# Second expert weights split by GpSimd, route weights formed once: one core, cross attention and mixture of experts

## The chip, the cores and the metric

One core of one Trainium2 chip runs the whole program. The metric is the device time in microseconds, of which three runs were made: median 615.03 us, from 614.83 to 616.17. The engines are TensorE (PE, with its weight loads PEld), VectorE (DVE), ScalarE (ACT), GpSimd (POOL) and SyncE (SP), which issues most transfers. They run side by side and order each other by semaphores; each works through its own instructions in their order.

## The reference, cut to what matters

The input x is 4 x 1024 rows of 256. Four blocks follow each other, each added to x with a tanh gain:

```
x = x + tanh(g_xattn[0]) * attention(layernorm(x), ctx, ctx, mask)     # 77 keys
x = x + tanh(g_ffn[0])   * moe(layernorm(x))                           # below
x = x + tanh(g_xattn[1]) * attention with projections, softmax over queries
x = x + tanh(g_ffn[1])   * gated feed-forward with integer weights

# moe, for xt = all 4096 rows
logits = xt @ gate_w.T + gate_b
scores = softmax(logits)
top_w, top_i = top_k(scores, 2)              # 8 experts, two for each row
y = sum over the two: top_w * ((silu(xt @ w1.T + b1) * (xt @ w3.T + b3)) @ w2.T + b2)
z = silu(xt @ ws1.T + bs1) * (xt @ ws3.T + bs3) @ ws2.T + bs2     # the shared expert
```

## The kernel before, in words

The rows are worked in 8 groups of 512 (NG = 8, GT = 4 tiles of 128 rows). Every product of the experts is made of three matmuls in a short format: each factor is split into a high part (a rounded copy, made by ScalarE with `copy`) and a low part (the rest, made by a subtraction), and high*high, high*low and low*high are added (`three`).

**Steps.** A loop over g = 1..7 (`step`, one function of this name on each engine) works at two groups together: the shared expert and the routing of group f = g - 1, and the first attention and second layer norm of group g, with the scores of group g + 1. The order on each engine is written out by hand. At the end of a step ScalarE runs, in this order: `hidden_high(f, 3)`, `route_exp(f)` (exp of 36 differences of logits per row, L891), `t2_copy(g)` (the high part of the transposed normed rows, n2Th), `softmax(g + 1)` (four Exp activations with a sum, L835), `expert_high(g)` (the high part of the second weights of expert g, w2h). The next step begins with `silu` (L861), then `pt_copy` (probsT), on which TensorE's `values` (L1294) waits. TensorE runs between its transposes `t2` (L1303) and those `values`: the rest of `down(f)`, then `up(0)`, `probs_t` (L1287, which waits for all probs), in some steps a small setup product, and `up(1)`.

VectorE ends a step with `row_max`, `t2_low`, `shared_out`, `ln1_stats(g + 2)`, then `route_c(f)` (five small instructions, L2084 to L2092: sum, reciprocal, gain, second weight, copy into gate_all) and `expert_low(g)` (L1943, w2l = stage - w2h, 128x512; in step 1 for experts 0 and 1). The next step begins with `prob_scale` (L1974), which needs the sums of the softmax, `hidden(f, 0)` and `residual1` (L2018), which needs `values`.

GpSimd in a step: `rstd_second(g)` (L601 and L604; nb2, on which ScalarE's `ln2_apply`, L815, waits), four scatters by indirect DMA, `rstd_first(g + 2)`, four more scatters. SyncE loads the three `stage` buffers in turn; the next load into one waits for the low part made from its contents (`low_done`).

**Behind the steps** comes the routing of the last group with tables of the expert tiles, then 40 expert tiles (31 of two row tiles, 9 of one), in which TensorE, ScalarE and VectorE work in a loop over u and GpSimd adds the bias (L674). gate_all is read only after them, by `x2`. b2 and b13 are loaded into the place of the buffers of the steps, `stage` among them.

**Activation tables.** In the program as compiled an ACT_TABLE_LOAD stands before an activation whose function is not in the loaded set; the profile shows it under the line of that activation. Exp and Silu lie in different sets, Copy and Identity in both.

Of the kernel before, what the change touches and what calls it, by code (L numbers as in the profile page):

```python
# [7 lines left out]
NE, F = 8, 256  # L8
SF, LF = 512, 768
DH, NH = 16, 16  # L10
P = 128
KD = D // P
T = B * S
GT = 4
NG = T // (P * GT)
# [32 lines left out]
def flamingo_kernel(nc, i, out):  # L48
    ctx = ExitStack()
    with ctx:  # L50
        sems = {}

        def sem(name):
            if name not in sems:
                sems[name] = ctx.enter_context(nc.semaphore(name))
            return sems[name]
# [64 lines left out]
        row_shift = keep.put("row_shift", [P, NE], F32)  # L121
        gate_all = keep.put("gate_all", [P, NG, 2, GT], F32)
        tile_expert = keep.put("tile_expert", [1, NU], I32)
        tile_row = keep.put("tile_row", [1, 2, NU], I32)
# [45 lines left out]
        top8i = w1.put("top8i", [P, GT, 8], U32)  # L170
        dlog = w1.put("dlog", [P, GT, NE + 1], F32)
        elog = w1.put("elog", [P, GT, NE + 1], F32)
        esum = w1.put("esum", [P, GT], F32)
        onehot = w1.put("onehot", [P, 2, GT, NE], F32)
# [3 lines left out]
        rsel = w1.put("rsel", [P, 2, GT, NE], F32)  # L178
        gatew = w1.put("gatew", [P, 2, GT], F32)
        pos = [w1.put(f"pos{p}", [P, 2, GT], U32) for p in range(2)]  # L180
# [174 lines left out]
        def _(sp):  # L355
            def small(dst, src, name="small_in"):
                sp.dma_start(dst, src).then_inc(sem(name), 16)
# [133 lines left out]
            sp.wait_ge(sem("u_done"), MS * NG)  # L491
            sp.wait_ge(sem("gate_done"), NG)
            small(b2, i["b2"].partition_broadcast(P), "b2_in")
            store_mid(7, 1)
# [6 lines left out]
            sp.wait_ge(sem("shared_done"), pairs(NG))  # L501
            sp.wait_ge(sem("route_kept"), 3 * NG)
            for u in range(NU):
# [53 lines left out]
        def _(pool):  # L557
# [57 lines left out]
            def shared_low(c, n):  # L615

                pool.wait_ge(sem(f"high_done{c % 3}"), n)
                pool.tensor_tensor(wsl[:, c, :], stage[c % 3], wsh[:, c, :], ALU.subtract).then_inc(sem(f"low_done{c % 3}"), 1)

            def scatter(f, p, ks=(0, 1), tiles=range(GT)):  # L620

                pool.wait_ge(sem("pos_done"), f + 1)
                for k in ks:
                    for j in tiles:
                        pool.indirect_dma_start(  # L625
                            out=xs, out_offset=bass.IndirectOffsetOnAxis(ap=pos[p][:, k, j:j + 1], axis=0),
                            in_=n2[p][:, j, :], in_offset=None).then_inc(sem(f"scattered{p}"), 16)
# [12 lines left out]
            rstd_first(0)  # L640
# [59 lines left out]

            pool.wait_ge(sem("route_kept"), 3 * NG)
            pool.wait_ge(sem("row_shift_done"), 1)
# [93 lines left out]
        def _(act):  # L796
# [120 lines left out]
            def step(g, p, nxt=True):  # L917
# [80 lines left out]
            silu(f, 3)  # L998
            route_exp(f)
            hidden_high(f, 3)  # L1000
# [246 lines left out]
        def _(pe):  # L1247
# [456 lines left out]

            pe.wait_ge(sem("table_done"), 3)
            experts = {0: expert_of(0)}
            tx(0)
# [196 lines left out]
        def _(dve):  # L1904
# [39 lines left out]

            def expert_low(g):
                low_part(g % 3, w2h[:, g, :], w2l[:, g, :], g // 3 + 3)

            def hidden_low(f, m):
# [114 lines left out]
            def route_a2(f):  # L2063
                dve.wait_ge(sem("top_done"), GT * (f + 1))
                m0 = top8[:, :, 0:1]
                tt(dlog[:, :, 0:NE], logit, m0.broadcast_to([P, GT, NE]), ALU.subtract)
                tt(dlog[:, :, NE:NE + 1], top8[:, :, 1:2], m0, ALU.subtract).then_inc(sem("dlog_done"), 1)

# [11 lines left out]

            def route_c(f):

                dve.wait_ge(sem("elog_done"), f + 1)
                dve.tensor_reduce(esum, elog[:, :, 0:NE], AX.X, ALU.add).then_inc(sem("weights_step"), 1)  # L2084
                dve.wait_ge(sem("weights_step"), 4 * f + 1)
                dve.reciprocal(esum, esum).then_inc(sem("weights_step"), 1)
                dve.wait_ge(sem("weights_step"), 4 * f + 2)
                ts(gatew[:, 0, :], esum, gains[:, 2:3], None, ALU.mult).then_inc(sem("weights_step"), 1)
                dve.wait_ge(sem("weights_step"), 4 * f + 3)
                tt(gatew[:, 1, :], gatew[:, 0, :], elog[:, :, NE], ALU.mult).then_inc(sem("weights_step"), 1)  # L2090
                dve.wait_ge(sem("weights_step"), 4 * f + 4)
                cp(gate_all[:, bass.ds(f, 1), :, :].rearrange("p a k j -> p (a k j)"), gatew.rearrange("p k j -> p (k j)"))\  # L2092
                    .then_inc(sem("route_kept"), 1)

# [23 lines left out]
            def step(g, p, nxt=True, more=True):  # L2118
# [175 lines left out]
            shift_kept()  # L2294
            route_c(f)
            weights_low(0)
# [45 lines left out]
            for u in range(NU + 1):  # L2342
                if u == KINDS.index("S"):
                    dve.wait_ge(sem("b13_in"), 16)
                if u < NU:
                    gated(u)
                if u < NU and not pair(u):
                    gated_single(u)
                if u + 2 < NU:
                    weights_low(u + 2)  # L2350
                if u and not pair(u - 1):
                    hidden_low_of(u - 1)
                if u + 2 < NU:
                    rows_low(u + 2)
                if u < NU and pair(u):
                    hidden_low_of(u)


# [115 lines left out]
            dve.wait_ge(sem("y_mm_done"), NU)  # L2474
            dve.wait_ge(sem("route_kept"), 3 * NG)

# [250 lines left out]
```

## Time and profile before

| | |
|---|---|
| median of three runs | 615.03 us |
| the profiled execution's own time | 614.06 us |
| its span, first to last instruction | 612.3 us |
| mean granted TensorE clock | 0.989 |
| busy: PE, PEld | 572.5 us (94%), 472.6 us (77%) |
| busy: DVE, ACT, POOL | 453.4 us (74%), 376.6 us (62%), 255.8 us (42%) |
| chain that ended last, by engine | PE 60%, DVE 18%, issue 7%, ACT 5% |

Busy time is the sum over an engine's instructions; matmuls are pipelined and their ends are modelled, so a busy PE is not PE at its peak. The chain is followed back from the last instruction, at each step to what released it. In a timeline a row gives the start, the duration, the engine, the line, the operation, the tiles and shapes and the count; in brackets stands how long the engine had been idle and what ended that. The steps lie between about 30 and 160 us of the span, the expert tiles between about 193 and 366 us.

### The profile page before, as it was taken

The page shows a single profiled execution, that of the slowest core. Times are in us where ns is not written, and L with a number is a line of the kernel's source. Part 1 is how long each engine was busy: PE and PEld are TensorE (multiplying, and loading weights), DVE is VectorE, ACT ScalarE, POOL GpSimd, SP SyncE. Part 2 cuts the span into 40 slices and gives each one's busy share as a digit, 9 for nine tenths or more (in the row PEclk, how much of TensorE's full clock was granted, in tenths as well). Part 3 has the DMA queues.
Part 4 walks back from the last instruction along what each step waited for, and adds up shares of the span by engine and source line. Part 5 has one row for each costly group of instructions (what it writes and reads, how often), then busy time and mean ns, then how long its engine had stood idle before and what let it go on. Part 6 is the DMA issues. An engine that isn't in the chain of part 4 may idle for free.

```text
span 612.3 us, 12917 instructions
## 1 busy us (share of the span) xinstructions
PE 572.5 (94%) x3956; PEld 472.6 (77%) x3956; DVE 453.4 (74%) x1246; ACT 376.6 (62%) x729; POOL 255.8 (42%) x284
## 2 busy tenths in 40 slices
PE   7889999998989999999999999699889989999997
PEld 7788889886769999999999988486645645655654
DVE  5888888885645877787798753567888798877755
ACT  5576777873435777777687653155574674684643
POOL 4445565553540235543353346577534650410100
PEclk9899999998999999999999999799999999999999
DMA  7334564441239768887988727632212340200000
GB/s 214 115 110 161 198 208 161 168 166 44 104 138 302 270 234 278 280 257 238 310 239 260 239 79 271 215 122 68 60 34 70 98 127 35 70 1 35 35 36 34
DMA packets 46005, 93.15 MB, mean 152 GB/s; under 512 B 6686, under 2 KB 15978, under 8 KB 45682
## 3 DMA queue, kind: packets, MB, share of 16 engines
q1 hardware_dynamic: 37868, 74.34, 35.9%
q0 software_dynamic: 7344, 17.97, 9.8%
q8 instruction: 33, 0.54, 0.4%
q14 instruction: 34, 0.28, 0.1%
q10 hardware_dynamic: 726, 0.02, 0.1%
HBM read 61.32 MB, written 32.17 MB: 153 GB/s over the span
## 4 chain that ended last, share of the span: by engine, by line
PE 60%; DVE 18%; issue 7%; ACT 5%; another core or an unknown queue 3%; DMA 3%; POOL 2%; SPq 2%; ACTq 0%; DVEq 0%; POOLq 0%
PE bank L1310 11%; PE bank L1308 11%; PE bank L1309 11%; PE bank L1809 6%; PE bank L1830 2%; DVE st L2385 2%; PE bank L1831 2%; PE bank L1652 2%; DMA wraw<-in_wexp 2%; DVE g3l L2462 2%; DVE xa L2376 2%; PE bank L1277 2%; DVE sl L2457 2%; PE bank L1294 2%
## 5 line engine op out<-in xcount | busy, mean ns | idle before, releaser
L625 POOL DMA_INDIRECT rows_by_expert<-n,pos x64 | 64.4, 1006 | 52.6 <-DVE pos L2113 36.1
L674 POOL TENSOR_TENSOR yg<-yg,b 128x512 f32<-128x512 f32 x31 | 46.4, 1498 | 93.9 <-ACT yg L798 93.9
L722 POOL DMA_INDIRECT yr<-expert_out,out_row x64 | 65.7, 1026 | 28.0 <-issue 19.4
L1809 PE MATMUL bank<-m4Th,wint 128*128 128x512 f16 x192 | 69.0, 380 | 5.3 <-DVE sl L2457 3.3
L1308 PE MATMUL bank<-xTh,wph 128*128 128x256 f32 x248 | 72.6, 293 | 1.1 <-DVE wpl L2278 1.0
L1310 PE MATMUL bank<-xTh,wpl 128*128 128x256 f32 x248 | 70.1, 283 | 0.0
L1309 PE MATMUL bank<-xTl,wph 128*128 128x256 f32 x248 | 70.0, 282 | 0.0
L1809 PE MATMUL bank<-m4Tl,wint 128*128 128x512 f16 x192 | 68.8, 379 | 0.0
L2278 DVE TENSOR_TENSOR wpl<-wraw,wph 128x1024 fp32r<-128x1024 f32 x40 | 49.0, 1225 | 14.7 <-ACT wph L798 14.5
L798 ACT ACTIVATE wph<-wraw 128x1024 fp32r<-128x1024 f32 x40 | 42.3, 1058 | 17.6 <-DMA wraw<-in_wexp 9.2
L2457 DVE SCALAR_TENSOR_TENSOR sl<-bank,sl 128x512 f32<-128x512 f32 x48 | 33.1, 689 | 22.5 <-ACT sl L1113 22.4
L1308 PEld LDWEIGHTS bank<-xTh,wph 128*128 128x128 f32 x248 | 47.4, 191 | 1.6 <-DVE wpl L2278 1.2
L1309 PEld LDWEIGHTS bank<-xTl,wph 128*128 128x128 f32 x248 | 47.5, 191 | 0.0
L1310 PEld LDWEIGHTS bank<-xTh,wpl 128*128 128x128 f32 x248 | 47.4, 191 | 0.0
L1830 PE MATMUL bank<-wint,g3h 128*128 128x256 f16 x192 | 42.9, 273 | 1.3 <-DVE g3l L2462 0.8
L1113 ACT ACTIVATE sl<-bank 128x512 f32<-128x512 f32 x48 | 28.3, 589 | 25.2 <-PE bank L1809 24.5
L1831 PE MATMUL bank<-wint,g3l 128*128 128x256 f16 x192 | 42.8, 272 | 0.0
L1308 PE MATMUL bank<-w2h,hTh 128*128 x142 | 40.2, 283 | 1.4 <-DVE hTl L2334 1.4
L1809 PEld LDWEIGHTS bank<-m4Th,wint 128*128 128x128 f16 x192 | 18.3, 98 | 29.1 <-DVE sl L2457 7.9
L1066 ACT ACTIVATE n<-xa,nb,rs 128x256 f32<-128x256 f32 x64 | 34.1, 589 | 10.9 <-DVE nb L2402 10.5
L1310 PE MATMUL bank<-w2h,hTl 128*128 x142 | 40.2, 283 | 0.0
L1309 PE MATMUL bank<-w2l,hTh 128*128 x142 | 40.2, 283 | 0.0
(351 smaller groups left out, 1753.8 us busy)
## 6 DMA issues: line engine op xcount, KB each, us to landing
wraw<-in_wexp SPq DMA_DIRECT2D x40, 512.0 KB
xg<-rows_by_expert SPq DMA_DIRECT2D x31, 256.0 KB, 4.0
expert_out<-yg SPq DMA_DIRECT2D x31, 256.0 KB, 2.9
x_shared<-x SPq DMA_DIRECT2D x8, 512.0 KB
xa<-x_shared SPq DMA_DIRECT2D x4, 1024.0 KB
out<-ost SPq DMA_DIRECT2D x8, 512.0 KB, 2.8
xin<-in_x SPq DMA_DIRECT2D x7, 512.0 KB, 3.8
stage<-in_wexp SPq DMA_DIRECT2D x8, 256.0 KB
```

What stands on the lines that cost most here:

```text
L625: pool.indirect_dma_start(out=xs, out_offset=bass.IndirectOffsetOnAxis(ap=pos[p][:, k, j:j + 1], axis=0), in_=n2[p][:, j, :], in_offset=No ...
L674: pool.tensor_tensor(yg[u % 3], yg[u % 3], b2[:, bass.ds(e, 1), :].broadcast_to([P, 2, D]), ALU.add)\
L722: pool.indirect_dma_start(out=yr[:, c, k, j, :], out_offset=None, in_=ys, in_offset=bass.IndirectOffsetOnAxis(ap=out_row[:, b * GB + c, k, ...
L798: return act.activation(dst, src, ACT.Copy)
L1308: mm(o, ah, bh, start=first, stop=False)
L1309: mm(o, ah, bl, start=False, stop=False)
L1310: return mm(o, al, bh, start=False, stop=final)
L1809: last = mm(bank[:, 2 * (m % 2) + w, :], wt[:, k, m * P:(m + 1) * P], part[c][:, k, :], start=(q == 0 and k == 0), stop=(q == 1 and k == K ...
L1830: mm(bank[:, j, 0:D], g3h[:, k, t], wdv[:, k, :], start=(k == 0), stop=False)
L1831: last = mm(bank[:, j, 0:D], g3l[:, k, t], wdv[:, k, :], start=False, stop=(k == ML - 1))
L2278: tt(wpl[u % 2], wraw[u % 3], wph[u % 2], ALU.subtract).then_inc(sem("low_done0"), 1)
L2457: stt(sl3[n % 3], bank[:, 2 * (m % 2) + 1, :], HID_SCALE, sl3[n % 3], ALU.mult, ALU.mult).then_inc(sem("g3_done"), 1)
```

## The change

The subtraction that makes w2l moves from the end of VectorE's step to the end of GpSimd's step. The route weights are no longer made group by group: `dlog` and `esum` get room for all eight groups, the differences are kept, one Exp activation over all 288 values per row stands where the last group's stood, in place, and four VectorE instructions (`route_weights`) behind tile u = 2 of the expert tiles write gate_all. So ScalarE has no `route_exp` in a step any more. SyncE, TensorE and VectorE get a few waits: b2's load and the first expert tile wait for the low parts, the first low parts of the tiles for those that GpSimd made on the same semaphore. The count of route_kept falls from three to two a group.

```diff
@@ gpsimd
+            def expert_low(g):
+                pool.wait_ge(sem(f"high_done{g % 3}"), g // 3 + 3)
+                pool.tensor_tensor(w2l[:, g, :], stage[g % 3], w2h[:, g, :], ALU.subtract).then_inc(sem(f"low_done{g % 3}"), 1)
...
                 scatter(f, 1 - p, (1,), first)
                 scatter(f, 1 - p, (1,), second)
+                if g == 1:
+                    expert_low(0)
+                expert_low(g)
@@ scalar
-            def route_exp(f):
-                act.wait_ge(sem("dlog_done"), f + 1)
-                act.activation(elog, dlog, ACT.Exp).then_inc(sem("elog_done"), 1)
+            def route_exp():
+                act.wait_ge(sem("dlog_done"), NG)
+                every = dlog.rearrange("p g j e -> p (g j e)")
+                act.activation(every, every, ACT.Exp).then_inc(sem("elog_done"), 1)
...
                 if g == 1:
                     expert_high(0)
-                route_exp(f)
                 t2_copy(g, (0,))
                 t2_copy(g, (1,))
...
             silu(f, 3)
-            route_exp(f)
+            route_exp()
             hidden_high(f, 3)
@@ vector
-            def route_c(f):
-                dve.wait_ge(sem("elog_done"), f + 1)
-                dve.tensor_reduce(esum, elog[:, :, 0:NE], AX.X, ALU.add).then_inc(sem("weights_step"), 1)
...
+            def route_weights():
+                dve.wait_ge(sem("elog_done"), 1)
+                dve.tensor_reduce(esum, dlog[:, :, :, 0:NE], AX.X, ALU.add).then_inc(sem("weights_step"), 1)
+                dve.wait_ge(sem("weights_step"), 1)
+                dve.reciprocal(esum, esum).then_inc(sem("weights_step"), 1)
+                dve.wait_ge(sem("weights_step"), 2)
+                ts(gate_all[:, :, 0, :], esum, gains[:, 2:3], None, ALU.mult).then_inc(sem("weights_step"), 1)
+                dve.wait_ge(sem("weights_step"), 3)
+                tt(gate_all[:, :, 1, :], gate_all[:, :, 0, :], dlog[:, :, :, NE], ALU.mult).then_inc(sem("weights_step"), 1)
...
-                route_c(f)
-                if g == 1:
-                    expert_low(0)
-                expert_low(g)
                 if g == 2:
...
             def weights_low(u):
                 dve.wait_ge(sem("high_done0"), EARLY[0] + u + 1)
+                dve.wait_ge(sem("low_done0"), EARLY[0] + u)
...
             shift_kept()
-            route_c(f)
             weights_low(0)
...
                     hidden_low_of(u)
+                if u == 2:
+                    route_weights()
@@ sync
+            for c in range(3):
+                sp.wait_ge(sem(f"low_done{c}"), EARLY[c])
             small(b2, i["b2"].partition_broadcast(P), "b2_in")
@@ tensor
             pe.wait_ge(sem("table_done"), 3)
+            for c in (1, 2):
+                pe.wait_ge(sem(f"low_done{c}"), EARLY[c])
```

## Rows read from the trace of the kernel before

**Rows 1.** Costliest groups on ScalarE by form, 0 to 190 us: busy us, mean ns
```profile
L861 ACT ACT_TABLE_LOAD x8 | 10.3, 1283 | 0.1
L891 ACT ACT_TABLE_LOAD x8 | 10.3, 1283 | 0.1
```

**Rows 2.** Timeline of ScalarE at the turn to step 6: start us, us
```profile
113.38 1.28 ACT L891 ACT_TABLE_LOAD   x1
...
114.81 1.07 ACT L798 ACTIVATE n2Th<-bank 128x512 fp32r<-128x512 f32 x2
...
117.24 0.23 ACT L835 ACTIVATION_READ_ACCUMULATOR probs<-bank,negmax,rstd 128x1 f32 x1
...
118.01 1.28 ACT L861 ACT_TABLE_LOAD   x1
...
119.71 0.58 ACT L798 ACTIVATE probsT<-bank 77x512 f32<-77x512 f32 x1
```

**Rows 3.** Timeline of TensorE at the same turn
```profile
113.45 1.03 PE L1303 MATMUL bank<-ident,n 128*128 128x128 f32 x8
...
117.85 0.60 PE L1287 MATMUL bank<-ident,probs 128*77 128x128 f32 x4
...
120.34 1.99 PE L1294 MATMUL bank<-ctxr,probsT 77*128 77x256 f32 x8 [0.65 <-ACT probsT L798]
```

**Rows 4.** Timeline of VectorE at the same turn
```profile
118.88 0.16 DVE L2084 TENSOR_REDUCE esum<-elog 128x4 f32<-128x32 f32 x1
...
120.43 0.17 DVE L1974 RECIPROCAL pscale<-psums 128x4 f32<-128x4 f32 x1
...
121.61 1.74 DVE L2018 SCALAR_TENSOR_TENSOR x<-bank,pscale,xin 128x256 f32<-128x256 f32 x4 [0.32 <-PE bank L1294]
```

**Rows 5.** ScalarE, turn to step 2
```profile
41.96 1.06 ACT L798 ACTIVATE n2Th<-bank 128x512 fp32r<-128x512 f32 x2
...
44.39 0.22 ACT L835 ACTIVATION_READ_ACCUMULATOR probs<-bank,negmax,rstd 128x1 f32 x1
```

**Rows 6.** TensorE, turn to step 2
```profile
40.42 1.03 PE L1303 MATMUL bank<-ident,n 128*128 128x128 f32 x8
...
44.96 0.60 PE L1287 MATMUL bank<-ident,probs 128*77 128x128 f32 x4
```

**Rows 7.** ScalarE, turn to step 3
```profile
62.86 0.23 ACT L835 ACTIVATION_READ_ACCUMULATOR probs<-bank,negmax,rstd 128x1 f32 x1
```

**Rows 8.** TensorE, turn to step 3
```profile
63.74 0.60 PE L1287 MATMUL bank<-ident,probs 128*77 128x128 f32 x4
```

**Rows 9.** ScalarE, turn to step 4
```profile
83.63 0.59 ACT L798 ACTIVATE probsT<-bank 77x512 f32<-77x512 f32 x1
```

**Rows 10.** TensorE, turn to step 4
```profile
84.28 1.99 PE L1294 MATMUL bank<-ctxr,probsT 77*128 77x256 f32 x8
```

**Rows 11.** TensorE, turn to step 5
```profile
102.37 0.92 PE L1294 MATMUL bank<-ctxr,probsT 77*128 77x256 f32 x3 [0.17 <-ACT probsT L798]
```

**Rows 12.** ScalarE, turn to step 7
```profile
135.35 0.22 ACT L835 ACTIVATION_READ_ACCUMULATOR probs<-bank,negmax,rstd 128x1 f32 x1
```

**Rows 13.** TensorE, turn to step 7
```profile
136.63 0.60 PE L1287 MATMUL bank<-ident,probs 128*77 128x128 f32 x4
```

**Rows 14.** ScalarE behind step 7
```profile
161.50 1.28 ACT L861 ACT_TABLE_LOAD   x1
166.90 0.69 ACT L861 ACTIVATE sil<-bank,bs 128x512 f32<-128x512 f32 x1 [4.11 <-remote]
```

**Rows 15.** GpSimd's bias add of the expert tiles: min, median, max ns
```profile
L674 POOL TENSOR_TENSOR yg<-yg,b x31: 1262/1301/2170, 205.4 to 364.1; 128x512 f32<-128x512 f32 x31
```

**Rows 16.** Timeline of GpSimd, step 6
```profile
126.72 0.20 POOL L604 TENSOR_TENSOR nb<-negm,rstd 128x4 f32<-128x4 f32 x1
```

**Rows 17.** Timeline of ScalarE, step 6, its use of nb2
```profile
128.74 1.08 ACT L815 ACTIVATE n<-x,nb,rstd 128x256 f32<-128x256 f32 x2
```

**Rows 18.** VectorE among the expert tiles
```profile
212.81 0.88 DVE L2314 SCALAR_TENSOR_TENSOR hb<-bank,b13c,hb 128x256 f32<-128x256 f32 x2 [0.77 <-PE bank L1310]
```

More of the change, by code:

```diff
@@ L122, in flamingo_kernel @@
         gate_all = keep.put("gate_all", [P, NG, 2, GT], F32)
+        dlog = keep.put("dlog", [P, NG, GT, NE + 1], F32)
+        esum = keep.put("esum", [P, NG, GT], F32)
         tile_expert = keep.put("tile_expert", [1, NU], I32)
@@ L170, in flamingo_kernel @@
         top8i = w1.put("top8i", [P, GT, 8], U32)
-        dlog = w1.put("dlog", [P, GT, NE + 1], F32)
-        elog = w1.put("elog", [P, GT, NE + 1], F32)
-        esum = w1.put("esum", [P, GT], F32)
         onehot = w1.put("onehot", [P, 2, GT, NE], F32)
@@ L178, in flamingo_kernel @@
         rsel = w1.put("rsel", [P, 2, GT, NE], F32)
-        gatew = w1.put("gatew", [P, 2, GT], F32)
         pos = [w1.put(f"pos{p}", [P, 2, GT], U32) for p in range(2)]
@@ L501, in _ @@
             sp.wait_ge(sem("shared_done"), pairs(NG))
-            sp.wait_ge(sem("route_kept"), 3 * NG)
+            sp.wait_ge(sem("route_kept"), 2 * NG)
             for u in range(NU):
@@ L699, in keep_rows @@
                 pool.wait_ge(sem("shifts_added"), NE + 1)
-            pool.wait_ge(sem("route_kept"), 3 * NG)
+            pool.wait_ge(sem("route_kept"), 2 * NG)
             pool.wait_ge(sem("row_shift_done"), 1)
@@ L1943, in low_part @@
                 tt(low, stage[c], high, ALU.subtract).then_inc(sem(f"low_done{c}"), 1)
-            def expert_low(g):
-                low_part(g % 3, w2h[:, g, :], w2l[:, g, :], g // 3 + 3)
             def hidden_low(f, m):
@@ L2065, in route_a2 @@
                 m0 = top8[:, :, 0:1]
-                tt(dlog[:, :, 0:NE], logit, m0.broadcast_to([P, GT, NE]), ALU.subtract)
-                tt(dlog[:, :, NE:NE + 1], top8[:, :, 1:2], m0, ALU.subtract).then_inc(sem("dlog_done"), 1)
+                tt(dlog[:, f, :, 0:NE], logit, m0.broadcast_to([P, GT, NE]), ALU.subtract)
+                tt(dlog[:, f, :, NE:NE + 1], top8[:, :, 1:2], m0, ALU.subtract).then_inc(sem("dlog_done"), 1)
             def route_b(f):
@@ L2079, in route_b @@
                 tt(routed, onehot[:, 0, :, :], onehot[:, 1, :, :], ALU.add).then_inc(sem("routed_done"), 1)
-            def route_c(f):
-                dve.wait_ge(sem("elog_done"), f + 1)
-                dve.tensor_reduce(esum, elog[:, :, 0:NE], AX.X, ALU.add).then_inc(sem("weights_step"), 1)
-                dve.wait_ge(sem("weights_step"), 4 * f + 1)
+            def route_weights():
+                dve.wait_ge(sem("elog_done"), 1)
+                dve.tensor_reduce(esum, dlog[:, :, :, 0:NE], AX.X, ALU.add).then_inc(sem("weights_step"), 1)
+                dve.wait_ge(sem("weights_step"), 1)
                 dve.reciprocal(esum, esum).then_inc(sem("weights_step"), 1)
[L2087 to L2093, printed above, removed]
+                dve.wait_ge(sem("weights_step"), 2)
+                ts(gate_all[:, :, 0, :], esum, gains[:, 2:3], None, ALU.mult).then_inc(sem("weights_step"), 1)
+                dve.wait_ge(sem("weights_step"), 3)
+                tt(gate_all[:, :, 1, :], gate_all[:, :, 0, :], dlog[:, :, :, NE], ALU.mult).then_inc(sem("weights_step"), 1)
             def route_d(f):
@@ L2474, in _ @@
             dve.wait_ge(sem("y_mm_done"), NU)
-            dve.wait_ge(sem("route_kept"), 3 * NG)
+            dve.wait_ge(sem("weights_step"), 4)
             chained(dve.memset(vscale, 0.0))
```

## The prediction

> **What bounds the kernel now.** I read the page first: TensorE is busy for nearly the whole span, VectorE for three quarters, so a gain on VectorE counts only where TensorE waits for it. Then I read, for the stretch of the steps, the costliest groups on ScalarE, since the change takes an Exp out of each step. The reader should see there eight table loads under the line of `route_exp` and eight under the line of `silu`, 1.28 us each [rows 1]: each step goes to the Exp set and back to the Silu set. None stands under the softmax, whose four activations are Exp as well, because `route_exp` has loaded the set just before. Last I read the timelines of the engines at the turn from one step to the next, step by step, because that is where both edits lie.
>
> At the turn to step 6 ScalarE loads the Exp set at 113.38, copies n2Th from 114.81, ends the softmax at 117.47, loads the Silu set at 118.01 and writes probsT from 119.71 to 120.29; TensorE's `values` start at 120.34 after an idle 0.65 us that probsT ended [rows 2, 3]. So here the loop is closed by ScalarE: TensorE's t2 ends at 114.48, and then t2_copy, softmax, expert_high, load, silu and probsT run one behind the other until `values`. VectorE's residual starts at 121.61, 0.32 us after VectorE had nothing left, and what ended the wait was `values` [rows 4]. VectorE has slack at this place, ScalarE has none.
>
> **The change, part by part.**
>
> *Exp leaves the step.* The source takes one activation of 36 elements away (about 0.15 us of ScalarE's time). The load in front of it does not go: the next Exp is the softmax of the same step, which now has to load the set itself. It moves from before t2_copy, where it lay beside TensorE's t2, to between t2_copy and the softmax, into the chain that `values` wait for. The gain against it is that t2_copy can start as soon as t2 ends. At the turn to step 6 that is 114.81 - 114.48 = 0.33 us, so the softmax ends later by 1.28 - 0.33 = 0.95 us [rows 2, 3]. Now each turn, with the slack that TensorE has in front of probs_t (it starts after the last probs are read) and in front of `values`:
>
> - Step 2: t2 ends at 41.45, t2_copy starts at 41.96, so the softmax is 1.28 - 0.51 = 0.77 late. It ended at 44.61, and probs_t started at 44.96: 0.35 of slack, 0.42 us come out [rows 5, 6].
> - Step 3: the softmax ended at 63.09, probs_t started at 63.74, slack 0.65. With 1.24 us of delay (t2_copy started 0.04 after t2 there, the smallest gap of the turns), 0.59 us come out [rows 7, 8].
> - Step 4: probsT is done at 84.22, `values` start at 84.28 [rows 9, 10]. No slack, and nearly the whole 1.24 us pass: 1.2 us.
> - Step 5: `values` waited 0.17 us for probsT [rows 11]. No slack; the delay lies between those of steps 4 and 6, I take 1.15 us.
> - Step 6: no slack either [rows 3]: 0.95 us.
> - Step 7: the softmax ended at 135.57, probs_t started at 136.63, slack 1.06, which covers a delay of about 1.0 [rows 12, 13], because TensorE has products of twice the width there: 0.
>
> Sum: 0.42 + 0.59 + 1.2 + 1.15 + 0.95 = 4.3 us. TensorE works through the rest of each step without a long pause, so what `values` lose isn't won back in the step.
>
> The bounds of this term: nothing, if the load were hidden after all, and 6 x 1.28 = 7.7 us, if each turn passed it on in full. I take 4.3, since each slack is read off at its own turn. The page "ScalarE: Activation LUTs" of the Trainium skill, section "What ACT_TABLE_LOAD costs", gives a drain of about 1380 ns on top of the 1283 ns of the load. This trace agrees on the load and does not show the drain: from the start of the load at 118.01 to the start of probsT at 119.71 there are 1.70 us, with the load and a silu in them [rows 2]. By the page's 2.66 us the five turns would cost 1.38 us more each, an estimate of about 11 us in all and somewhat over 1 us more in step 7.
>
> *Two switches less.* Step 7 has no softmax behind it, so its Exp load and the Silu load in front of the last group's silu go away. The second one ran from 161.50 to 162.78, and the silu behind it started at 166.90 after 4.11 us of idling [rows 14]: worth nothing. The first stood before a t2_copy that waited for TensorE. I take 0; if both were bare, -2.6 us. In the last group the Exp grows from 36 to 288 elements a row; it is 0.2 us longer, before a hidden_high that TensorE's `down` reaches late. 0, at most +0.2.
>
> *VectorE loses 1.55 us a step*: from the start of esum at 118.88 to that of pscale at 120.43 [rows 4]. The new pscale can start at 118.88, since the softmax, now later, ends at 117.47 + 0.95 = 118.42. But the residual waits for `values`, so all of it turns into idle time in the turns where TensorE or ScalarE comes last. Value 0.
>
> *GpSimd gains one subtraction of 128x512 a step, two in step 1.* The nearest row is its add of the same size: 1.26 to 2.17 us, median 1.30 [rows 15]; I take 1.4. It is queued behind eight scatters and ahead of rstd_second, so nb2 comes later by as much, and ScalarE's n2 waits for nb2. In step 6 nb2 was done at 126.92 and n2 started at 128.74: slack 1.82 [rows 16, 17]. 1.4 fits, and 2.17 as well, since ScalarE itself comes about 1 us later by then. In step 2 two subtractions, 2.8 us, meet a slack of about that kind and 0.4 us of the new delay: n2 may be about 0.6 us late, which TensorE's t2 does not feel. I take 0; the upper end is 2 x 2.17 less 1.8 and 0.4, 2.1 us. SyncE's next load into a stage buffer waits for GpSimd and holds the load of x behind it for some 3 us in step 2, but x is wanted a good part of a step later.
>
> *route_weights at u = 2.* Four small instructions on VectorE. Their nearest rows are the old five, which took 0.95 us a group (118.88 to 119.83); the sum now reads eight times as many elements, so it is at most 8 x 0.16 = 1.3 us instead of 0.16 [rows 4]. That makes 0.9 to 2.1 us, I take 1.2. It lies beside TensorE's tile; VectorE idled 0.77 us at u = 4 for TensorE [rows 18], and its low parts are made two tiles ahead. Value 0, at most 1.2 where the cover fails. The new waits of SyncE, TensorE and VectorE ask for work done long before: 0.
>
> **The sum** is made on the profiled execution's own time: 614.06 + 4.3 = 618.4 us. The median of the three runs is 0.97 above that, so I forecast 615.03 + 4.3 = 619.3 us.
>
> **The rivals.** A measurement of this kernel tells about 0.2%, 1.2 us, from no change.
>
> 1. *The load stays hidden* (it is placed earlier, or I take the wrong chain as the last). Then the turns give nothing back but ScalarE's small gaps: 0.17 and at most 0.33 us in steps 5 and 6. 614.5 to 615.3 us, the same as before. Against it: all 16 loads stand right before the activation that needs them. Chance 0.10.
> 2. *Faster: VectorE closes the loop at the turns.* Place: the residual at the start of a step. If VectorE came last there, each turn could be 1.55 us shorter; with the load in the chain as well, I take half of that over five turns, -3.9 us: 611.1 us. It decides where VectorE did not idle before the residual; at the turn to step 6 it idled [rows 4], so it would have to hold for the other turns. Chance 0.07. In its favour speaks the same page of the Trainium skill, section "Table sets: the hidden batching unit": batching the calls by set saves switches, and this change does save two of sixteen. By rows that is at most 2.6 us, and [rows 14] say it is 0.
> 3. *GpSimd becomes the late one as well*: its subtraction takes 2 us beside VectorE, and nb2 holds up n2 in several steps. +1 to +3 us on top: 620.3 to 622.3. Chance 0.07.
> 4. *A later wait swallows part of the delay.* Behind step 7 ScalarE idled 4.11 us for something that the trace does not name [rows 14]. If the end of such a wait is not tied to the steps before, up to 3 us of the delay vanish: 616.3 to 618 us. Chance 0.11.
>
> **How the numbers follow.** Forecast as it stands, 617.8 to 621 us: 0.65. The range goes down to 615.8, which takes in most of rival 4, and up to 622, which takes in rival 3 and the low end of the full 7.7 us. Slower: 0.65 + 0.07 + 0.10 of rival 4 = 0.82. Same: 0.09. Faster: 0.09, rival 2 and a little for what I do not see.
>
> **What would show it.** Right: six table loads under the line of the softmax, none between `hidden_high(f, 3)` and t2_copy; seven under `silu`; TensorE idling about 1 to 1.8 us before `values` in steps 4 to 6 and about 0.5 before probs_t in steps 2 and 3; VectorE idling longer before the residual; the expert tiles as long as before. Wrong: the turns as long as they were (rival 1), the steps shorter with VectorE's residual early (rival 2), ScalarE's n2 waiting for nb2 (rival 3), or steps 2 to 6 longer by 4.3 us and the whole not (rival 4).

## The result and the profile after

| | changed kernel | kernel before, beside it |
|---|---|---|
| median | 623.07 us (619.73 to 624.03, 4 runs) | 615.6 us (614.83 to 617.26, 4 runs) |
| profiled execution | 623.86 us, span 622.1 us | 614.06 us, span 612.3 us |
| mean granted TensorE clock | 0.991 | 0.989 |
| ratio | 1.0105 (95% interval 1.0061 to 1.0149) | |

The change makes the kernel slower by 7.5 us by the medians and by 6.5 us by the ratio (3.8 to 9.2 by its interval). I had forecast 619.3 us and a range up to 622.0, so the sign is right and the size too small. In the profiled executions the difference is 9.8 us.

The groups of ScalarE from 25 to 165 us, after (line, engine, operation, count, busy us, mean ns, idle us before them), answer to [rows 1]:

```profile
L823 ACT ACTIVATE n<-x,nb,rstd 128x256 f32<-128x256 f32 x30 | 16.2, 588 | 0.0
...
L869 ACT ACT_TABLE_LOAD x7 | 9.0, 1283 | 0.1
L843 ACT ACT_TABLE_LOAD x6 | 7.7, 1283 | 0.1
```

L843 is the softmax and L869 the silu: six loads stand under the softmax, none under a small Exp, as forecast. The first row shows that ScalarE's `n2` never waited for GpSimd's nb2.

ScalarE at the turn to step 6, after, answers to [rows 2]:

```profile
121.82 1.08 ACT L806 ACTIVATE n2Th<-bank 128x512 fp32r<-128x512 f32 x2 [1.50 <-PE bank L1311]
122.92 1.28 ACT L843 ACT_TABLE_LOAD   x1
124.22 0.42 ACT L843 ACTIVATE probs<-bank,negmax,rstd 128x77 f32<-128x77 f32 x1
...
125.71 0.21 ACT L843 ACTIVATION_READ_ACCUMULATOR probs<-bank,negmax,rstd 128x1 f32 x1
125.80 0.63 ACT L806 ACTIVATE w2h<-stage 128x512 fp32r<-128x512 f32 x1
126.45 1.28 ACT L869 ACT_TABLE_LOAD   x1
127.74 0.47 ACT L869 ACTIVATE sil<-bank,bs 128x256 f32<-128x256 f32 x1
128.12 0.58 ACT L806 ACTIVATE probsT<-bank 77x512 f32<-77x512 f32 x1
```

TensorE and VectorE at the same turn, after, answer to [rows 3] and [rows 4]:

```profile
125.97 0.66 PE L1295 MATMUL bank<-ident,probs 128*77 128x128 f32 x4 [0.66 <-issue]
...
128.75 0.48 PE L1302 MATMUL bank<-ctxr,probsT 77*128 77x256 f32 x1 [0.87 <-ACT probsT L806]
```

```profile
130.02 1.74 DVE L2025 SCALAR_TENSOR_TENSOR x<-bank,pscale,xin 128x256 f32<-128x256 f32 x4 [1.28 <-PE bank L1302]
```

The load stands between n2Th and the softmax. TensorE waits twice in the turn, 0.66 us for the last probs (the row says "issue", but the last probs are read at 125.92 and it starts at 125.97) and 0.87 us for probsT. So the idle time that I had forecast before `values` comes in two parts, in steps 4 to 6: 0.66 us before probs_t and 0.55 to 0.87 us before `values`. VectorE, relieved of 1.55 us, waits 1.28 us for `values`, where it waited 0.32 us before [rows 4].

To add this up I took, for each step, the start of TensorE's t2 and of its `values` in both traces. The turn from t2 to `values` grew by 0.74, 0.89, 1.41, 1.27, 1.11 and 0.22 us in the turns to steps 2 to 7, 5.64 us in all. From `values` to the next t2 the steps grew by 1.0 us in all, of which step 2 has 0.92. That makes 6.6 us. The other 3.2 us of the two profiled executions are 1.66 us at the very start, before any changed instruction (TensorE waited 0.84 us for the first rows of x), 0.24 us behind the steps and 1.28 us among the expert tiles. The start varies in this way from execution to execution (in the profiles of the experiments the `values` of group 1 begin between 26.42 and 29.85 us, in kernels that change nothing up to there), so I don't count it to the change.

Why step 2 is longer is seen on GpSimd and VectorE. After, step 2, GpSimd, VectorE, ScalarE and TensorE:

```profile
53.98 2.52 POOL L623 TENSOR_TENSOR w2l<-stage,w2h 128x512 fp32r<-128x512 f32 x2
56.61 1.22 POOL L601 TENSOR_TENSOR rstd<-ve,halfpow 128x4 f32<-128x4 f32 x1
```

```profile
55.04 0.36 DVE L1938 BATCH_NORM_AGGREGATE mv<-st 128x2 f32<-128x6 f32 x4
55.44 1.09 DVE L1944 TENSOR_SCALAR ve<-mv 128x4 f32<-128x4 f32 x1
56.44 0.16 DVE L1945 TENSOR_SCALAR negm<-mv 128x4 f32<-128x4 f32 x1
56.51 0.41 DVE L1958 TENSOR_TENSOR hl<-sil,hh 128x256 fp32r<-128x256 f32 x1
```

```profile
57.02 0.47 ACT L869 ACTIVATE sil<-bank,bs 128x256 f32<-128x256 f32 x1 [2.62 <-DVE hl L1958]
```

```profile
58.83 0.67 PE L1285 MATMUL bank<-ctxC,n1T 128*128 128x77 f32 x4 [0.89 <-ACT n1T L806]
```

`ve`, four elements wide, takes 1.09 us and ends when the pair of subtractions ends (53.98 + 2.52 = 56.50). The same instruction in the kernel before took 0.17 us in each of its seven executions. Next but one in VectorE's order stands `hl` (`hidden_low(f, 0)`), for which ScalarE's `silu(f, 2)` waits; behind that comes n1T, for which TensorE's scores wait 0.89 us. These waits for n1T are 0.89, 0.21, 0.36, 0.35 and 0.37 us in steps 2 to 6, 2.2 us in all, where the kernel before had 0.40 us in step 4 and 0.23 us in step 6. The 1.0 us above is smaller, because those two are gone and because step 7 happens to be 0.47 us shorter.

Not everything on VectorE is held. The four BATCH_NORM_AGGREGATE that stand just before `ve` run inside the subtractions and take 0.36 us together, as they do in the kernel before.

### The profile page after: what moved, and what is told of

Its sections match the earlier page's. It is cut to its first block, busy times and chain, and to the rows that moved or that the text cites. A ratio compares the mean times of both kernels' runs of the same rounds, so it can differ in the third digit from the quotient of the medians.

```text
span 622.1 us, 12914 instructions
## 1 busy us (share of the span) xinstructions
PE 577.0 (93%) x3956; PEld 474.2 (76%) x3956; DVE 445.3 (72%) x1202; ACT 372.8 (60%) x720; POOL 266.2 (43%) x292
## 4 chain that ended last, share of the span: by engine, by line
PE 52%; DVE 20%; issue 11%; ACT 7%; DMA 4%; SPq 2%; POOL 2%; another core or an unknown queue 1%; ACTq 0%; DVEq 0%; POOLq 0%
PE bank L1316 10%; PE bank L1317 9%; PE bank L1318 9%; PE bank L1819 5%; PE bank L1840 2%; PE bank L1841 2%; DVE st L2387 2%; PE bank L1660 2%; PE bank L1285 2%; DVE xa L2378 2%; DVE g3l L2464 2%; DVE x L2025 2%; DVE sl L2459 2%; DMA wraw<-in_wexp 2%; DVE st L2031 1%
## 5 line engine op out<-in xcount | busy, mean ns | idle before, releaser
L740 POOL TENSOR_SCALAR ve<-mv 128x4 f32<-128x4 f32 x16 | 5.2, 324 | 84.3 <-DVE mv L2391 80.1
```

## The experiments

Twelve kernels were run, each beside the kernel before on the same chip, in three groups on three chips: the kernel before had a median of 598.06 us beside the first four, of 598.36 us beside the next four and of 615.4 us beside the last four. So times count within a group; between groups I compare the difference from the kernel before, and the turns inside a profile, which chips don't change much (the changed kernel's turns to steps 4 and 5 are 8.01 and 8.00 us in both of its profiles, on two chips). Step 7 is an exception: from `values` to t2 it is 16.16 us long in the kernel before and 15.69 us in the changed one, on the first chip, both with a granted clock of 0.50 for some three microseconds in it, and 12.90 us in the changed kernel's second profile, where the clock is 1.00 there. Each table gives the difference from the kernel beside it twice, by the ratio and by the medians.

Two theories stood against each other at first. A: the cost is the table load in the chain of the turn. S: GpSimd's subtraction costs too, by its own queue (a late nb2) or by holding up something else.

### The load alone, the subtraction alone, and each taken back

**e2_load_late**: the kernel before with route_exp behind t2_copy.

```diff
-                route_exp(f)
                 t2_copy(g, (0,))
                 t2_copy(g, (1,))
+                route_exp(f)
```

> The kernel before with route_exp moved behind t2_copy, so that only the table load moves between t2_copy and the softmax; VectorE and GpSimd do what they did. Theory A: +5.5 us to +6.5 us (the 5.6 us of the turns and 0.1 us of the Exp itself in each). If VectorE's relief paid for a part of the load in the changed kernel, more than that: up to +8 us. Rival B: no change.

**e4_weights_once**: the changed kernel with `expert_low(g)` back on VectorE.

```diff
@@ gpsimd
-                if g == 1:
-                    expert_low(0)
-                expert_low(g)
@@ vector
+                if g == 1:
+                    expert_low(0)
+                expert_low(g)
```

> The changed kernel with the low parts w2l back on VectorE; the route weights are formed once. Theory A: the turns as long as in the changed kernel, step 2 shorter by 0.9 us: +4.5 to +6.5 us against the kernel before. Rival B: within 1 us of the kernel before.

**e3_low_gpsimd**: the kernel before with only the subtraction moved to GpSimd (and the waits that go with it).

```diff
                 scatter(f, 1 - p, (1,), second)
+                if g == 1:
+                    expert_low(0)
+                expert_low(g)
```

> The kernel before with only the low parts w2l moved to GpSimd; the route weights stay in the steps. Theory A: the load stays hidden, and what is left is the wait of VectorE's ve beside GpSimd's subtraction, 0.9 us in step 2 and at most 0.2 in each other: +0.3 to +2 us. Rival B: +5 us or more. Rival C (VectorE's relief of 0.6 us a step is worth something): -0.5 to -2 us.

**e1_exp_back**: the changed kernel with a small Exp of one group back in front of t2_copy, its result unused, so that the load is covered again.

```diff
                     expert_high(0)
+                group_exp(f)
                 t2_copy(g, (0,))
```

> The changed kernel with one small Exp of the group's 36 differences back in each step, in front of t2_copy; its result goes to a tile that nobody reads, so the only use of it is that the Exp set is loaded there. Theory A (the table load in front of the softmax is the cause): the turns come back to 8.1, 7.5, 6.6, 6.7, 6.9 and 8.3 us from t2 to values, the time falls by about 5.6 us against the changed kernel, to 0.5 to 2 us above the kernel before; what is left is GpSimd's share. Rival B (GpSimd's subtraction and its port are the cause): no fall, 6 to 8 us above the kernel before.

| | median us | ratio (95%) | difference us |
|---|---|---|---|
| e2_load_late | 604.72 | 1.0104 (1.0078 to 1.0130) | 6.2, 6.7 |
| e4_weights_once | 605.65 | 1.0115 (1.0086 to 1.0144) | 6.9, 7.6 |
| e3_low_gpsimd | 613.56 | 1.0255 (1.0228 to 1.0282) | 15.3, 15.5 |
| e1_exp_back | 613.01 | 1.0257 (1.0230 to 1.0284) | 15.4, 15.0 |

The load alone costs 6.2 us or somewhat more, which bears out theory A. The turns of e2_load_late are 0.87, 0.71, 1.53, 1.55, 1.53 and 0.34 us longer than those of d1_pow_delay below, whose median is that of the kernel before: 6.5 us. But from `values` to t2 its steps are 1.7 us shorter, since TensorE's scores no longer wait for n1T there (0.40 us in step 4 and 0.65 us in step 5 of d1_pow_delay), so 4.9 us of the 6.2 are found in the steps. The rest is not placed.

What I had not expected is the size of the second pair, far outside what I had written for theory A. With the load covered, the subtraction on GpSimd costs 15 us. Putting the small Exp back did not heal the changed kernel, it made it worse. VectorE, GpSimd, ScalarE and TensorE in e1_exp_back, step 5:

```profile
113.73 1.70 DVE L1950 TENSOR_SCALAR ve<-mv 128x4 f32<-128x4 f32 x1
115.34 0.16 DVE L1951 TENSOR_SCALAR negm<-mv 128x4 f32<-128x4 f32 x1
115.42 0.41 DVE L1964 TENSOR_TENSOR hl<-sil,hh 128x256 fp32r<-128x256 f32 x1
```

```profile
114.10 1.30 POOL L624 TENSOR_TENSOR w2l<-stage,w2h 128x512 fp32r<-128x512 f32 x1
115.51 1.22 POOL L602 TENSOR_TENSOR rstd<-ve,halfpow 128x4 f32<-128x4 f32 x1
```

```profile
115.92 0.47 ACT L870 ACTIVATE sil<-bank,bs 128x256 f32<-128x256 f32 x1 [3.51 <-PE bank L1324]
116.30 0.40 ACT L807 ACTIVATE hh<-sil 128x256 fp32r<-128x256 f32 x1
116.60 1.07 ACT L807 ACTIVATE n1T<-bank 128x512 f32<-128x512 f32 x2
```

```profile
117.73 0.67 PE L1291 MATMUL bank<-ctxC,n1T 128*128 128x77 f32 x4 [1.80 <-ACT n1T L807]
```

`ve` waits until the subtraction is over (114.10 + 1.30 = 115.40). Then comes `hl`, then `silu(f, 2)` after 3.51 us of idle ScalarE (the row names TensorE, which had been done; what came last is `hl`), then n1T, and TensorE's scores after 1.80 us of idle. And it doesn't end there. The windows of e1_exp_back around that pause (us, busy time and count of PE, PEld, DVE, ACT, POOL, then granted clock, DMA share, GB/s):

```profile
116.00:118.00 2.00, 0.27 (x2) 0.27 (x3) 1.93 (x19) 1.68 (x4) 0.93 (x2) 1.00 0.04 14
118.00:120.00 2.00, 2.00 (x19) 2.00 (x19) 1.27 (x8) 1.91 (x5) 0.00 (x0) 0.86 0.02 4
120.00:122.00 2.00, 2.00 (x17) 1.94 (x17) 1.82 (x10) 1.98 (x4) 0.43 (x1) 0.50 0.00 0
122.00:124.00 2.00, 2.00 (x16) 2.00 (x16) 0.37 (x2) 0.68 (x2) 1.70 (x2) 0.79 0.18 66
```

After two microseconds in which TensorE was busy for 0.27, the granted clock falls from 1.00 to 0.50, which is 1.2 instead of 2.4 GHz, and comes back some four microseconds later. So the 1.5 us that `ve` loses in step 5 lengthen the way from `values` to t2 from 11.61 us (d1_pow_delay) to 14.29 us. In steps 4 to 6 of e1_exp_back this stretch is 14.09 to 14.32 us long, against 11.01 to 11.61.

The two parts of the price can be told apart. In steps 2 and 3 of e1_exp_back `ve` takes 1.96 and 1.32 us, the clock is not lowered behind the pause, and the stretch is 1.64 and 1.14 us longer than in d1_pow_delay: what `ve` lost, within 0.2 us. In steps 4 to 6 `ve` takes 2.00, 1.70 and 2.01 us, the granted clock falls to 0.50 each time, and the stretch is 2.72, 2.68 and 3.31 us longer, 0.9 to 1.5 us more than `ve` lost. So some 8.1 of the 11.5 us by which these five steps grew are `ve` held, and the 3.4 us above that stand in the steps with the low clock. Which pause the clock follows isn't settled: step 2 here has one of 1.77 us and step 4 of e3_low_gpsimd one of 1.80 us, and both keep a clock of 1.00 in the two microseconds after it.

### GpSimd's queue, or VectorE held

**a1_changed_again** is the changed kernel once more, for a number on the same chip as the next three. The 6.6 and 15.5 us in what I expected of it were measured on the chip of the first four.

> The changed kernel once more, on the chip of the runs beside it. Theory P (two causes that don't add: the Exp set's load behind t2_copy, 5.6 us over the turns, and GpSimd's subtraction, which holds up VectorE's ve; the later turns keep most of ve clear of it): 6 to 8 us above the kernel before. Theory Q (causes add up): as on this chip the load alone gave 6.6 us and the subtraction alone 15.5 us, it would be 20 us or more.

**d1_pow_delay**: the kernel before with a small power (128x4) on GpSimd where the subtraction would stand. It delays rstd_second and nb2 as a subtraction does, but reads almost nothing.

```diff
                 scatter(f, 1 - p, (1,), second)
+                pool.tensor_tensor(idle_pow, mean_of[:, 0:GT], halfpow[:, 0:GT], ALU.pow)
```

> The kernel before with one power of 4 values a row (about 1.05 us on GpSimd, next to no data) where the change puts the subtraction. Its result is not read. Theory P (what costs is that ve is held while GpSimd reads 128x512): ve stays at 0.17 us, values to t2 stays at 11 us, time within 1 us of the kernel before. Rival S (what costs is GpSimd's queue, nb2 late by about a microsecond): values to t2 about 14 us, +10 us or more.

**f1_low_in_gap**: e3_low_gpsimd with the subtraction moved behind rstd_second of the next step, where GpSimd waits for pos.

```diff
                 rstd_second(g)
+                if g > 1:
+                    if g == 2:
+                        expert_low(0)
+                    expert_low(g - 1)
                 scatter(f, 1 - p, (0,), first)
```

> As e3_low_gpsimd (only the low parts on GpSimd), but each subtraction stands behind rstd_second of the next step, in the 4.4 us in which GpSimd waits for the positions. Theory P (it is the place beside ve that costs): ve takes 0.17 us again, values to t2 is 10.8 to 11.4 us again, the time is -1 to +1.5 us against the kernel before. Rival R (VectorE suffers wherever GpSimd subtracts): +5 us or more.

**f2_both_in_gap**: the same move in e1_exp_back, so the whole change with the load covered and the subtraction in the gap.

> The whole change with both costs taken out: the small Exp stays in the step in front of t2_copy, and the subtraction stands in GpSimd's gap behind rstd_second. Theory P: -1.5 to +1 us against the kernel before (VectorE has 1.55 us less in each step, but TensorE sets the pace). Rival R: +5 us or more.

| | median us | ratio (95%) | difference us |
|---|---|---|---|
| a1_changed_again | 607.42 | 1.0152 (1.0126 to 1.0178) | 9.1, 9.1 |
| d1_pow_delay | 598.63 | 1.0007 (0.9990 to 1.0023) | 0.4, 0.3 |
| f1_low_in_gap | 603.58 | 1.0085 (1.0060 to 1.0110) | 5.1, 5.2 |
| f2_both_in_gap | 603.51 | 1.0080 (1.0057 to 1.0102) | 4.8, 5.2 |

The changed kernel lies above the 6 to 8 us of theory P (its interval is 7.5 to 10.7 us), and far below the 20 us of theory Q. A delay of GpSimd's queue by 1.04 to 1.23 us costs nothing that can be measured (-0.6 to 1.4 us), so theory S in its first form falls, and the second form is left. `ve` in d1_pow_delay, step 5, beside the power on GpSimd:

```profile
107.28 0.17 DVE L1936 TENSOR_SCALAR ve<-mv 128x4 f32<-128x4 f32 x1
```

```profile
107.31 1.05 POOL L640 TENSOR_TENSOR idle_pow<-mean_of,halfpow 128x4 f32<-128x4 f32 x1
```

`ve` starts ahead of the power here, and so it does ahead of the subtraction in e1_exp_back. The closest pair is step 6 of d1_pow_delay and step 4 of e1_exp_back, where `ve` starts 0.67 us before GpSimd's instruction in both, while GpSimd's last scatter still runs:

```profile
124.84 0.25 DVE L1936 TENSOR_SCALAR ve<-mv 128x4 f32<-128x4 f32 x1
125.51 1.04 POOL L640 TENSOR_TENSOR idle_pow<-mean_of,halfpow 128x4 f32<-128x4 f32 x1
```

```profile
92.57 2.00 DVE L1950 TENSOR_SCALAR ve<-mv 128x4 f32<-128x4 f32 x1
93.24 1.29 POOL L624 TENSOR_TENSOR w2l<-stage,w2h 128x512 fp32r<-128x512 f32 x1
```

So it is not the scatter that holds `ve`: what differs is the instruction behind it. Why `ve` is held before the subtraction is recorded, the rows don't tell; GpSimd's spans are rough.

By their time f1_low_in_gap and f2_both_in_gap are a miss for theory P and the figure of rival R. In the gap `ve` is free again (0.17 us in all seven of f1_low_in_gap), but the subtraction found another victim. f1_low_in_gap, step 5, GpSimd, VectorE and ScalarE:

```profile
111.60 1.27 POOL L625 TENSOR_TENSOR w2l<-stage,w2h 128x512 fp32r<-128x512 f32 x1
```

```profile
112.05 0.86 DVE L2077 TENSOR_TENSOR dlog<-logit,top 128x32 f32<-128x32 f32 x1
```

```profile
113.42 0.42 ACT L810 ACTIVATE hh<-sil 128x256 fp32r<-128x256 f32 x1 [1.11 <-DVE sil L2048]
...
116.23 0.40 ACT L810 ACTIVATE hh<-sil 128x256 fp32r<-128x256 f32 x1
116.65 1.28 ACT L903 ACT_TABLE_LOAD   x1
```

The difference of logits, 0.17 us in each step of d1_pow_delay and 0.86 to 1.11 us in steps 2 to 6 here, ends when the subtraction does (112.87 and 112.91). `hidden(f, 2)` comes later by 0.7 us, ScalarE waits 1.11 us for it, and its last hh and the load behind it slide along, so that n2Th starts at 118.08, 0.61 us after t2 is done at 117.47. So the turns to steps 4 to 6 are 0.6 us longer than in d1_pow_delay (7.20 against 6.59 or 6.60). All turns and steps together are 3.1 us longer than in d1_pow_delay; the other 2 us of the measured 5.1 are not placed. And f1 and f2 are equal: forming the weights once is worth nothing.

### What the pieces of the turn are worth

**g1_weights_hidden**: e4_weights_once with the small Exp kept in front of t2_copy (as in e1_exp_back). VectorE's relief stands alone.

> Route weights formed once among the expert tiles, but the 36-element Exp stays in front of t2_copy and the low parts stay on VectorE. So VectorE's relief of 0.95 us a step stands alone. Theory T (VectorE's time before pscale is covered, its residual waits for TensorE's values): 0 to -0.6 us against the kernel before, that is 597.8 to 598.4 us. Rival V (VectorE closes the loop at the turns): -3 us or more, under 595.5 us.

**g2_low_quarters**: e3_low_gpsimd with the subtraction cut in four.

```diff
-                pool.tensor_tensor(w2l[:, g, :], stage[g % 3], w2h[:, g, :], ALU.subtract)
+                for q in range(4):
+                    n = slice(q * P, (q + 1) * P)
+                    ins = pool.tensor_tensor(w2l[:, g, n], stage[g % 3][:, n], w2h[:, g, n], ALU.subtract)
```

> The kernel before with only the subtraction on GpSimd, at the same place as in e3_low_gpsimd, but cut into four of 128x128. Theory H (a small VectorE instruction that meets the subtraction is held until the GpSimd instruction in hand ends): ve is held for at most one quarter, 0.3 to 0.7 us instead of 1.0 to 2.3, and the time comes down from +15 us to +2 to +7, 600 to 605 us. Rival W (the two engines share the way to memory for as long as GpSimd works, however it is cut): ve stays at 1 to 2 us and the time at +13 to +16 us, 611 to 614 us.

**g3_high_behind** and **g4_exposed_behind**: g1_weights_hidden and e4_weights_once with `expert_high` out of the chain, and its low part one step later.

```diff
@@ scalar
                 silu(f, 1)
+                if g > 1:
+                    expert_high(g - 1)
                 hidden_high(f, 0)
...
                     softmax(g + 1, second)
-                expert_high(g)
@@ vector
-                if g == 1:
-                    expert_low(0)
-                expert_low(g)
+                expert_low(g - 1)
```

> g1_weights_hidden, with expert_high moved behind probsT and silu(f, 1) of the next step and its low part one step later on VectorE. It takes 0.65 us out of the chain softmax, expert_high, load, silu, probsT. Theory A (ScalarE closes the loop only in steps 5 and 6 of the kernel before, by 0.2 to 0.65 us of idle TensorE): -0.3 to -1.3 us against the kernel before. Rival B (another engine is right behind, so nothing comes): 0. Slower by more than 1 us only if expert_high delays hidden_high(f, 0).

> e4_weights_once (load exposed in front of the softmax, low parts on VectorE), with expert_high moved in the same way. Theory A (in steps 3 to 6 the exposed load stands in a chain that is closed by ScalarE, so each 0.65 us taken out of it comes back in full): 4 or 5 times 0.5 to 0.65 us, -2 to -3.2 us against e4_weights_once's +6.9, so +3.7 to +4.9 us over the kernel before, 602 to 603.3 us. Rival B (the exposed load costs by something other than this chain): the time stays at +6 to +7 us.

| | median us | ratio (95%) | difference us |
|---|---|---|---|
| g1_weights_hidden | 615.87 | 0.9999 (0.9969 to 1.0028) | -0.1, 0.5 |
| g2_low_quarters | 629.82 | 1.0229 (1.0163 to 1.0296) | 14.1, 14.4 |
| g3_high_behind | 615.50 | 0.9985 (0.9956 to 1.0014) | -0.9, 0.1 |
| g4_exposed_behind | 618.35 | 1.0026 (0.9993 to 1.0058) | 1.6, 3.0 |

g1 shows VectorE's relief at nothing, within 1.9 us either way: theory T. In its profile the residual of the turn to step 6 waits 1.28 us for `values`.

g2 goes against the theory I had written it for. g2_low_quarters, step 5, GpSimd and VectorE:

```profile
113.36 1.97 POOL L627 TENSOR_TENSOR w2l<-stage,w2h 128x128 fp32r<-128x128 f32 x4
```

```profile
112.78 1.90 DVE L1949 TENSOR_SCALAR ve<-mv 128x4 f32<-128x4 f32 x1
113.12 1.57 DVE L1950 TENSOR_SCALAR negm<-mv 128x4 f32<-128x4 f32 x1
114.60 0.41 DVE L1963 TENSOR_TENSOR hl<-sil,hh 128x256 fp32r<-128x256 f32 x1
```

The four quarters together last longer than the whole (1.97 against 1.30 us here, 1.68 to 1.97 us over the steps), and `ve` is not let in behind the first of them: it ends at 114.68, within the third quarter by an even split, so two or three quarters went first. In step 2, with eight quarters, it took 2.40 us. Over the seven steps its median is 1.66 us, where theory H wanted 0.3 to 0.7, and the time is rival W's. Cutting the subtraction is no remedy; whether `ve` was held to the end of one quarter that happened to be late, or passed over several times, the rows don't tell, since GpSimd's spans are rough (`ve` starts 0.58 us before the first quarter is recorded).

In g3 TensorE's `values` in the turn to step 6 still wait 0.50 us for probsT. What follows the load is now another wait:

```profile
118.03 1.28 ACT L862 ACT_TABLE_LOAD   x1
120.00 0.47 ACT L862 ACTIVATE sil<-bank,bs 128x256 f32<-128x256 f32 x1 [0.69 <-PE bank L1318]
120.38 0.58 ACT L799 ACTIVATE probsT<-bank 77x512 f32<-77x512 f32 x1
```

The silu in front of probsT waits 0.69 us for TensorE's `up(0)`. The 0.65 us taken out by the move reappear there: my rival B. With the load exposed (g4) ScalarE is later, the silu does not wait, and the turns to steps 4 to 6 go from 8.01 to 7.50 us, 0.5 us each. That is theory A's sign, though the time lies below the 3.7 to 4.9 us that I expected. The rest of g4's profile can't be used for a sum: it is the slowest of its twelve executions (621.41 us), with a granted clock near 0.50 from 68 to 78 us, a turn to step 3 of 9.28 us (8.36 in e4_weights_once) and 14.35 us from there to t2 (10.84). By the ratios g4 lies 1.6 us above the kernel before (-0.4 to 3.6) and e4 6.9 us (5.1 to 8.6). The three turns explain 1.5 us of it, which is just the distance between the near ends of the two intervals; whether more came back stays open.

No kernel of the twelve was faster than the kernel before beyond its interval.

## Why the prediction was right, and where it was wrong

**The load.** Right in mechanism: where it goes, that step 7 and the last group pay next to nothing, and what TensorE waits for. The load alone, e2_load_late, costs 6.2 us (4.7 to 7.8); the term was 4.3. Each turn was undersized by 0.1 to 0.3 us:

| turn to step | 2 | 3 | 4 | 5 | 6 | 7 | sum |
|---|---|---|---|---|---|---|---|
| forecast | 0.42 | 0.59 | 1.2 | 1.15 | 0.95 | 0 | 4.3 |
| measured | 0.74 | 0.89 | 1.41 | 1.27 | 1.11 | 0.22 | 5.64 |

I took a load at its own duration, 1.28 us. From the start of n2Th to that of the first probs it is 124.22 - 121.82 = 2.40 us after. In d1_pow_delay, which has no load there, it is 115.66 - 114.69 = 0.97 us. So a load put between two activations costs 1.43 us: two of them overlap by about 0.1 us at their ends, and with a load in between they don't. At step 6 n2Th follows t2's end by 0.04 us, so 0.29 of the 0.33 us come back, and 1.43 - 0.29 = 1.14 us against 1.11 measured. In steps 2 and 3, besides, probs_t starts 0.05 us behind the last probs, which my slack had left out. At step 7 the slack of 1.06 us did not quite cover the load. One premise failed the other way: I had said that what `values` lose isn't won back in the step, and with the load exposed alone, in e2_load_late, the steps win back some of it (10.95 us from `values` to t2 in steps 4 to 6, against 11.36, 11.08 and 11.21 in the kernel before). "What ACT_TABLE_LOAD costs" in the page "ScalarE: Activation LUTs" of the Trainium skill had 2.66 us with the drain; the trace shows 1.43 us, so the drain I had set aside is not there, and what I missed is the small overlap.

**The subtraction on GpSimd, "I take 0".** This is the step that failed. Its duration was nearly right (1.275 to 1.305 us measured, 1.4 taken), and so was the slack of nb2: `n2` had no idle time, d1_pow_delay shows such a delay to be free, and rival 3 did not come about. But I had costed GpSimd's queue only, and looked for the damage behind it (rival 3). The damage is on VectorE: `ve`, or dlog where the subtraction is moved, is held until the subtraction ends. In the changed kernel `ve` takes 1.09 us in step 2 and has a median of 0.55 us over the steps; TensorE's waits for n1T that follow are 2.2 us, of which 1.0 us is left as net growth between `values` and t2. The 2.2 us are also the distance of a1_changed_again (9.1 us) from e4_weights_once (6.9 us), though the two stood on different chips and their intervals overlap. My bound of 2.1 us from above was just about reached in the changed kernel, and it holds for nothing else: with the load covered the same subtraction costs 15 us. The Trainium skill states a rule in the page "SBUF — State Buffer", section "SBUF: two separate sides": a GpSimd operation and a VectorE operation that has two SBUF inputs or runs in a 2-port mode take a shared pair of ports as an exclusive lock for the whole instruction, and the one that comes second blocks. The runs agree in part: dlog (two inputs, 0.17 to 1.11 us) and `ve` (one input, 0.17 to 2.30 us) end with the subtraction, and the BATCH_NORM_AGGREGATE before `ve` is not held. They don't show in what mode `ve` runs, and two things don't fit: `ve` is held although it is recorded ahead of the subtraction, and beside the power of 128x4, which GpSimd computes for 1.05 us, `hl` with its two inputs starts at 107.46, inside it, and takes its usual 0.41 us. That it is this lock and not another is the page's word; no run took the ports apart.

**The two parts don't add.** By themselves they cost 6.2 and 15 us, together 9.1 us, all on chips where the kernel before takes 598 us (6.5 us, 3.8 to 9.2, on the first chip). The exposed load makes the residual and so `ve` about a microsecond later against GpSimd's scatters, and by then most of the subtraction is over (0.55 us held instead of 1.70). The changed kernel, step 5, subtraction and `ve`:

```profile
113.28 1.28 POOL L623 TENSOR_TENSOR w2l<-stage,w2h 128x512 fp32r<-128x512 f32 x1
```

```profile
114.06 0.55 DVE L1944 TENSOR_SCALAR ve<-mv 128x4 f32<-128x4 f32 x1
```

It starts 0.78 us into the subtraction, where in e1_exp_back it stood ahead of it; TensorE's wait for n1T is 0.35 us in that step, and the granted clock is 1.00 in each window of 2 us from 115 to 123 us. So both parts of the price shrink, the hold and what the low clock adds to it.

**VectorE's relief, 0.** Right: g1_weights_hidden, f1 against f2, and the residual that waits 1.28 us for `values`. Rival 2 falls with it. **route_weights, 0.** Right in size (216.72 to 218.05 us, 1.3 us against 1.2 taken), and g1_weights_hidden, which has it too, costs nothing. **Rival 1**, the load stays hidden: no. **Rival 4**, a later wait swallows the delay: no, TensorE's first expert tile comes 8.5 us later in the profile after, against 8.3 us at t2 of step 7.

So 4.3 + 0 should have been 5.6 us in the turns and, net, 1.0 us in the steps, which gives 621.7 us by my own sum. The median lies 1.4 us above that, within the interval of its ratio.

## What to carry to other kernels

Taking an activation out of a loop does not take its table load out; look for the next activation of that set, because the load will stand there, and price it with the overlap it breaks (1.43 us here, not 1.28). When elementwise work goes to GpSimd, list what VectorE executes in that time, the smallest instructions first, and follow what is queued behind them; GpSimd's idle time says nothing about this price. And test two parts of a change one by one: here one part hid four fifths of the cost of the other, and taking the visible fault back would have made the kernel slower.

## What was not expected of the hardware

- A VectorE instruction of four elements a row (`ve`) took 1.00 to 2.30 us instead of 0.17 beside GpSimd's subtraction of 128x512 (e1_exp_back, e3_low_gpsimd), and 0.41 to 1.09 us where it came later against it (the changed kernel); beside a GpSimd power of 128x4, 0.17 to 0.25 us.
- Four subtractions of 128x128 one behind the other took 1.68 to 1.97 us, one of 128x512 1.30 us, and they let VectorE in no sooner (median of `ve` 1.66 us, against 1.23 us in e3_low_gpsimd).
- In e1_exp_back TensorE was busy for 1.93 of the 2 us from 114, then for 0.27 of 2 us with a clock of 1.00; it worked on without a pause and was granted 0.86, 0.50 and 0.79 in the next three windows and 1.00 from 124 us on. One pause of 1.80 us so cost more than itself. The changed kernel's pauses of 0.35 to 0.87 us around step 5 were followed by 1.00. The clock can fall with less: in g4_exposed_behind TensorE was busy for 1.51 and 1.82 us in the two windows of 2 us before 68 us, and was granted about 0.50 for the next ten microseconds.
